# Tensor product pass: the edges of the first 136 destinations by dense one-hot sums, the gathered path in 42 rounds instead of 49

## The reference, cut to what matters

```python
h = jnp.maximum(_layernorm(x, axis=-1), 0.0)
x = x + _L1_gnn_ref(h, edge_index, edge_attr_9, L1_gnn_w0, ..., L1_gnn_w4)
...
summand = _tensor_product(x[i], edge_attr, [w0, w1, w2, w3, w4])     # i: source of the edge
out = jax.ops.segment_sum(summand, j, num_segments=x.shape[0])       # j: destination
```

## Time and profile before

| what | value |
|---|---|
| median of 3 executions | 5813.45 us (5812.42 to 5815.08) |
| span of the profiled execution | 5807.9 us; the median lies 5.55 us above it |
| busy over the span | PE 4154.3 us, DVE 2538.0, ACT 2396.3, POOL 4025.0 |
| tensor pass, first to last gather | 1036.8 to 2996.3 us |
| in that pass (1036 to 3010 us) | PE busy 1292.19 us, POOL 1481.96, DVE 411.88, ACT 379.40; granted clock of TensorE 0.78 |
| granted clock | mean 0.779 over the span |

### The profile page before, as it was taken

One profiled execution on the slowest core, in us unless ns is written; L12 is line 12 of the kernel. 1 busy time (PEld: TensorE's weight loads), 2 busy tenths in 40 slices (PEclk: granted clock), 3 DMA queues, 4 the chain that ended last, 5 costly groups with the idle time before them and its releaser, 6 DMA issues. The chain is left out here.

```text
span 5807.9 us, 96744 instructions
## 1 busy us (share of the span) xinstructions
PE 4154.3 (72%) x26855; PEld 3465.6 (60%) x26855; DVE 2538.0 (44%) x8212; ACT 2396.3 (41%) x5947; POOL 4025.0 (69%) x4127
## 2 busy tenths in 40 slices
PE   3299996566666666666666777777777777659995
PEld 2167664456656656565555666666666666546664
DVE  5898665212222222222235555555555555542224
ACT  1645554212112111121136776666666666530113
POOL 0267775677777777777756777777777777557774
PEclk7599997777778777778776767667666777679998
DMA  4134443222222222222223333333333333255552
GB/s 70 41 126 147 168 155 122 65 57 56 57 57 56 57 56 57 57 56 57 57 50 78 85 83 79 85 79 83 85 77 85 84 78 85 59 175 173 172 173 71
DMA packets 363883, 510.14 MB, mean 88 GB/s; under 512 B 200193, under 2 KB 258822, under 8 KB 352705
## 3 DMA queue, kind: packets, MB, share of 16 engines
q0 software_dynamic: 129536, 268.78, 18.2%
q1 hardware_dynamic: 231785, 238.76, 13.3%
q10 hardware_dynamic: 2400, 0.57, 0.1%
HBM read 416.50 MB, written 91.05 MB: 87 GB/s over the span
## 5 line engine op out<-in xcount | busy, mean ns | idle before, releaser
L3202 POOL DMA_INDIRECT rows_l<-table,idx_l x1568 | 1481.6, 945 | 511.5 <-issue 470.9
L2831 POOL DMA_INDIRECT rows_l<-table,idx_l x1568 | 1482.0, 945 | 497.2 <-issue 477.6
L1533 POOL DMA_INDIRECT rows_l<-table,row_idx x896 | 944.8, 1054 | 303.2 <-issue 271.8
L2972 PE MATMUL ps_l<-hoty_l,rows_l 128*128 128x144 f32 x3136 | 724.6, 366 | 335.8 <-DMA rows_l<-table,idx_l 278.8
L2852 ACT COPY agg_l<-ps_l 128x288 f32<-128x288 f32 x784 | 312.3, 398 | 1548.4 <-PE ps_l L2972 1547.7
L3490 PE MATMUL banks_l<-wrow_l,hot_l 128*128 128x136 f32 x3136 | 709.7, 397 | 276.5 <-ACT hot_l L3576 275.6
L3490 PEld LDWEIGHTS banks_l<-wrow_l,hot_l 128*128 128x128 f32 x3136 | 649.4, 296 | 343.9 <-issue 218.2
L2972 PEld LDWEIGHTS ps_l<-hoty_l,rows_l 128*128 128x128 f32 x3136 | 552.0, 239 | 417.5 <-DMA rows_l<-table,idx_l 268.3
L2898 DVE TENSOR_TENSOR hoty_l<-p_hot_l,y_l 128x1152 f32<-128x1152 f32 x196 | 266.0, 1357 | 913.8 <-PE ps_l L2972 803.0
L2987 PE MATMUL pm_l<-w_mix,agg_l 128*128 128x128 f32 x3528 | 637.4, 318 | 0.4 <-ACT msg_l L2863 0.4
L2987 PEld LDWEIGHTS pm_l<-w_mix,agg_l 128*128 128x128 f32 x3528 | 588.2, 235 | 7.5 <-ACT msg_l L2863 0.6
(11 more groups left out here) (565 smaller groups left out, 6992.9 us busy)
## 6 DMA issues: line engine op xcount, KB each, us to landing
rows_l<-table,idx_l POOLq DMA_INDIRECT x3136, 2.5
e_l<-in_edge_attr SPq DMA_DIRECT2D x196, 256.0 KB
counts_table<-x_nodes SPq DMA_DIRECT2D x22, 1568.0 KB
x_nodes<-counts_table SPq DMA_DIRECT2D x22, 1568.0 KB
counts_table<-h_nodes SPq DMA_DIRECT2D x21, 1568.0 KB
h_nodes<-counts_table SPq DMA_DIRECT2D x21, 1568.0 KB
rows_l<-table,row_idx POOLq DMA_INDIRECT x896
raw_l<-in_edge_attr SPq DMA_DIRECT2D x49, 144.0 KB
```

The source lines that it names most:

```text
L1533: pool.indirect_dma_start(out=rows[:, slot, j, :], out_offset=None, in_=table, in_offset=bass.IndirectOffsetOnAxis(ap=what[:, j:j + 1], ax ...
L2831: pool.indirect_dma_start(out=rows[:, u, j, :], out_offset=None, in_=table, in_offset=bass.IndirectOffsetOnAxis(ap=idx[:, u, j:j + 1], axi ...
L2972: last = nc.tensor.matmul(ps[q][:, at:at + Y * RANGE], rows[:, u, 2 * q + i, :], hoty[:, s, 2 * q + i, :, :].rearrange("p c d -> p (c d)") ...
L3202: pool.indirect_dma_start(out=rows[:, u, j, :], out_offset=None, in_=table, in_offset=bass.IndirectOffsetOnAxis(ap=idx[:, u, j:j + 1], axi ...
```

## The change

The first 28 groups (28,672 edges) are no longer gathered: the loop over groups runs over the last 168, now written out without a hardware loop (`PassGroup`). Instead the first 136 destinations are computed apart, 29,502 edges on average; of those past edge 28,672 the one-hot places in the gathered path are pushed out of range (`done_far`).

- A destination gets a fixed number of visits (`caps`, its mean count of edges plus 4.5 deviations, in tiles of 128): 22, 10, 8, 7, 6, 6, 5, ... 2, together 372 in 8 batches of 17 destinations (106, 52, 44 and five of 34).
- Two visits at a time, DVE makes one-hots of the source's low 7 bits (`d_hot`, 128x256) and of its high part (`d_high`, 128x98), and multiplies the latter by 9 attributes (`d_row`, 128x882). PE multiplies them (128x441 f32) and sums over the visits in the PSUM bank `pd`: this is the count of the destination over all 49x128 nodes for each attribute. ACT copies it to `d_sums`.
- For each batch 49 matmuls (128x153) with `core.h` in 7 slices sum h by those counts, ACT copies to `d_agg`, 9 small matmuls mix, DVE adds to `acc`.
- `plan` lays these pieces (372 visits, 56 slices, 8 mixes, 32 empty) over the 672 slots, from slot 32 to 12 before the end, at most one in a slot. The piece stands behind `sums` and `mix` of its slot on PE.
- SP loads sources and attributes of each destination by two DMAs (`load_dense`), one or several groups ahead. DVE prepares each batch by 22 small operations (`prepare`).
- A new small stage `dense_stage` works out where each destination's edges begin. If a destination has more edges than its visits hold, or the 136 have under 28,672, or edges are unsorted, the flag `num[0:1, 0:1]` makes the pass run twice, first over groups 28 to 195, then over 0 to 167, and the dense part counts nothing.
- The node stage of layer 1 writes to `core.h` in place of a double buffer `tab`.
- `pw` and `py` share a bank, so `turn_raw` is one piece in slot 0 of a round's second group, and `y` has two buffers.

```diff
+    NODES, BATCH, SKIP = 136, 17, 7
+    RUN, RING, SLICES, FIRST, TAIL = 2, 6, 7, 32, 12
...
+        self.caps = []
+        for i in range(self.NODES):
+            many = sh.e * (((i + 1) / sh.n) ** 0.5 - (i / sh.n) ** 0.5)
+            self.caps.append(int(-(-(many + 4.5 * many ** 0.5) // P)))
...
+        pieces, gaps = [], 0
+        for b in range(self.batches):
+            for i in range(b * self.BATCH, (b + 1) * self.BATCH):
+                for v in range(self.first[i], self.first[i + 1]):
+                    pieces.append(("visit", i, v))
+            pieces.append(None)
+            for k in range(self.SLICES):
+                pieces.append(("apply", b, k))
+            pieces.append(None)
+            pieces.append(("mix", b, 0))
+            pieces += [None, None]
+        self.groups = (self.sh.rounds - self.SKIP) * U
+        self.parts = J // 2
+        slots = self.groups * self.parts
+        room = slots - self.FIRST - self.TAIL
+        assert len(pieces) <= room
+        self.at = [[] for _ in range(slots)]
+        for n, piece in enumerate(pieces):
+            if piece is not None:
+                self.at[self.FIRST + n * room // len(pieces)].append(piece)
...
+            link(nc.vector.tensor_tensor_scan(ends[:, :], ones[:, :], many[:, :], 0.0, ALU.mult, ALU.add))
+            nc.vector.tensor_tensor(begins[:, :], ends[:, :], many[:, :], ALU.subtract)
...
+            nc.vector.tensor_scalar(num[0:1, 1:2], ends[0:1, N - 1:N], float(dense.skipped) - 0.5, None, ALU.is_lt)
+            link(nc.vector.tensor_scalar(num[0:1, 2:3], core.order[0:1, 1:2], 0.5 * FAR, None, ALU.is_lt))
+            link(nc.vector.tensor_tensor(num[0:1, 0:1], num[0:1, 0:1], num[0:1, 1:2], ALU.max))
...
+            nc.vector.tensor_scalar(num[0:1, 3:4], num[0:1, 0:1], -1.0, 1.0, ALU.mult, ALU.add)
...
+            def load_dense(w, i):
+                k = dense.caps[i]
+                first = dense.place_of(dense.first[i])
+                cols = slice(first, first + k)
+                if i % B == 0 and dense.batch_of(i) >= 2:
+                    sp.wait_ge(dense_hot, START + w * (V // RUN) + dense.columns(dense.batch_of(i) - 2).stop // RUN)
+                    sp.sem_inc(batch_begun, 1)
+                at = ds(sp.value_load(dense.starts[0:1, i:i + 1], min_val=0, max_val=sh.e - dense.most * P), k * P)
+                loaded = dense_loaded[dense.batch_of(i)]
+                sp.dma_start(d_src[:, cols], src[at].rearrange("(p j) -> p j", j=k)).then_inc(loaded, DMA)
+                sp.dma_start(d_attr[:, cols, :].rearrange("p j c -> p (j c)"),
+                             attr[at, :].rearrange("(p j) c -> p (j c)", j=k)).then_inc(loaded, DMA)
...
+            def take_dense(w, slot):
+                for kind, n, k in dense.done_before(slot):
+                    if kind == "visit" and k == dense.first[n + 1] - 1:
+                        act.wait_ge(dense_counted, START + w * V + k + 1)
+                        if n >= B:
+                            act.wait_ge(batch_applied, START + w * dense.batches + dense.batch_of(n))
+                        nc.scalar.copy(d_sums[:, :, :, n % B].rearrange("p a c -> p c a"),
+                                       pd[:, 0:wide].rearrange("p (c a) -> p c a", a=A)).then_inc(node_taken, 1)
+                    if kind == "apply" and k == dense.SLICES - 1:
...
+                        if n:
+                            act.wait_ge(batch_mixed, START + w * dense.batches + n)
+                        nc.scalar.copy(d_agg[:, :], pd[:, 0:Y * B]).then_inc(batch_taken, 1)
...
+            def hots_of_nodes(v, w):
+                at, mine = v % RING, dense.place_of(v)
+                if v >= RING:
+                    dve.wait_ge(dense_counted, START + w * V + v + RUN - RING)
+                dve.wait_ge(dense_hot, START + w * (V // RUN) + v // RUN)
+                nc.vector.tensor_tensor(d_high, steps[:, 0:A].unsqueeze(1).broadcast_to([P, RUN, A]),
+                                        d_hi[:, mine:mine + RUN].unsqueeze(2).broadcast_to([P, RUN, A]), ALU.is_equal).then_inc(dense_high, 1)
+                nc.vector.tensor_tensor(d_hot[:, at:at + RUN, :], steps.unsqueeze(1).broadcast_to([P, RUN, P]),
+                                        d_lo[:, mine:mine + RUN].unsqueeze(2).broadcast_to([P, RUN, P]), ALU.is_equal)
+                dve.wait_ge(dense_high, START + w * (V // RUN) + v // RUN + 1)
+                nc.vector.tensor_tensor(d_row[:, at:at + RUN, :, :], d_high.unsqueeze(2).broadcast_to([P, RUN, Y, A]),
+                                        d_attr[:, mine:mine + RUN, :].unsqueeze(3).broadcast_to([P, RUN, Y, A]), ALU.mult).then_inc(dense_hot, 1)
...
+            def turn_raw(t, k):
+                pe.wait_ge(raw_loaded, START + t * DMA + DMA)
+                if k is not None:
+                    pe.wait_ge(added, START + k)
+                pe.sem_inc(turn_begun, 1)
+                for c in range(Y):
                     last = nc.tensor.transpose(py[:, c * tiles:(c + 1) * tiles],
                                                raw[:, :].rearrange("t (e c) -> t c e", c=Y)[:, c, :], core.ident[0:tiles, 0:tiles])
-                if end == Y:
-                    last.then_inc(raw_turned, 1)
+                last.then_inc(raw_turned, 1)
...
+            def count_visit(w, i, v):
+                if v == dense.first[i]:
+                    if i:
+                        pe.wait_ge(node_taken, START + w * N + i)
+                    if i % B == 0 and dense.batch_of(i):
+                        pe.wait_ge(batch_added, START + w * dense.batches + dense.batch_of(i))
+                if v % RUN == 0:
+                    pe.wait_ge(dense_hot, START + w * (V // RUN) + v // RUN + 1)
+                nc.tensor.matmul(pd[:, 0:wide], d_hot[:, v % RING, :], d_row[:, v % RING, :, :].rearrange("p c a -> p (c a)"),
+                                        start=(v == dense.first[i]), stop=(v == dense.first[i + 1] - 1)).then_inc(dense_counted, 1)
...
+            def apply_batch(w, b, k):
+                first, end = A * k // dense.SLICES, A * (k + 1) // dense.SLICES
+                if k == 0:
+                    pe.wait_ge(node_taken, START + w * N + (b + 1) * B)
+                for a in range(first, end):
+                    last = nc.tensor.matmul(pd[:, 0:Y * B], core.h[:, a, :], d_sums[:, a, :, :].rearrange("p c i -> p (c i)"),
+                                            start=(a == 0), stop=(a == A - 1))
+                if end == A:
+                    last.then_inc(batch_applied, 1)
...
+            def dense_part(w, slot):
+                for kind, n, k in dense.at[slot]:
+                    if kind == "visit":
+                        count_visit(w, n, k)
+                    elif kind == "apply":
+                        apply_batch(w, n, k)
+                    else:
+                        mix_batch(w, n)
+            with pe.Fori(0, windows) as w:
+                turn_raw(w * R, None)
+                for g in groups_of(w):
                     for q in range(PAIRS):
-                        mix(g, q)
-                    place_sums(g.near(-1))
...
-                edge_loop(sh, pe, w, body)
+                        sums(g, q)
+                        mix(g.near(-1), q)
+                        if q == 1:
+                            place_sums(g.near(-2))
+                        if q == 0 and g.u == 1 and g.rnd < R - 1:
+                            turn_raw(g.t + 1, g.near(-3).k + 1 if g.near(-3) else None)
+                        dense_part(w, slots(g)[q])
+                    if g.near(1) is None:
+                        for q in range(PAIRS):
+                            mix(g, q)
+                        place_sums(g.near(-1))
+                        place_sums(g)
```

More of the change, by code:

```diff
@@ L2714, in tensor_pass @@
         tiles = U * J
-        full, rest = divmod(sh.e - (R - 1) * U * GROUP, P)
-        assert 0 < full < tiles and tiles == 32
+        full, rest = divmod(sh.e - (sh.rounds - 1) * U * GROUP, P)
+        assert 0 < full < tiles and tiles == 32 and R % 2 == 0
+        V, B, N, RUN, RING = dense.visits, dense.BATCH, dense.NODES, dense.RUN, dense.RING
+        seen, skipped_tiles = dense.seen_tiles, dense.SKIP * U * J
+        A = sh.blocks
+        wide = Y * A
+        assert wide <= 512 and Y * B <= 512
         rel = sb("rel", [P, G, J])
@@ new lines, in mix_batch @@
+            def mix_batch(w, b):
+                pe.wait_ge(batch_taken, START + w * dense.batches + b + 1)
+                for c in range(Y):
+                    last = nc.tensor.matmul(pd[:, 0:B], w_mix[:, c, :], d_agg[:, c * B:(c + 1) * B], start=(c == 0), stop=(c == Y - 1))
+                last.then_inc(batch_mixed, 1)
+            def dense_part(w, slot):
[6 more added lines that the diff above has]
+                        mix_batch(w, n)
```

473 lines of the change are left out of this document (347 added, 126 removed).

## The result

| | median of 4 executions | lowest to highest |
|---|---|---|
| before | 5812.93 us | 5808.65 to 5815.08 |
| changed | 5538.39 us | 5536.97 to 5545.04 |

The ratio is 0.9531, 95% interval 0.9517 to 0.9545: faster by 274.5 us. The forecast was 5547 us, range 5536 to 5600. The span of the profiled execution is 5536.5 us (before 5807.9), the mean granted clock 0.812 (0.779).

What follows compares the result with a forecast made beforehand. POOL's back-to-back gathers were taken to set the pass, all else beside them. Terms -280 + 8 + 3 + 0 + 1 + 2 = -266 us took the span from 5807.9 to 5541.9; plus 5.55 gave 5547 us, range 5536 to 5600.

Steps and rivals of the forecast that it cites:

- The bound and the main term: Pass: POOL's gathers set the time; 224 fewer gathers at 1.250 us each save 280.0 us.
- PE fits: Pass: PE's 1147 us at full clock plus 70 of waits fit POOL's 1680 us, at a clock of 0.8 or more.
- Waits: Pass: PE waits for ACT's copy out of `pd`, 0.66 us at 135 places, 0 to 89 us, taken as 70.
- `raw`: PE's wait for attributes each round grows from 6.9 to 9.4 us, less for a late PE; it costs nothing.
- DVE: Pass: a pair of visits takes 1.75 us; DVE needs 721 of 1680 us in all and stays hidden.
- POOL disturbed: Pass: DVE's small preparations lengthen the gathers they meet, 0 to 5 us, taken as 2 us.
- Fixed costs: Outside the gathers: `dense_stage` 8 us (5 to 15), start of the pass 3 (1 to 7), end 0.
- A backlog of PE at the end: End of the pass: dense work left on PE could last to the end, 1 us, bounds 0 to 12.
- The sum: Whole kernel: the terms add to -266 us, span 5541.9 us; with 5.55 us from span to median, 5547 us.
- PE behind in part: Rival in the pass: at clock 0.70 PE needs 1728 us against 1680, 48 us more, 5595 us; chance 15%.
- the half clock rival: Rival in the pass: PE at half clock becomes the bound, about 2530 us, total 6397 us; chance 3%.
- The pass ran once: Rival on the whole pass: the flag fires and the pass runs twice, 7227 us; chance 1%.

Runs made afterwards that it cites:

- 41, 42 and 44 rounds: Gathered rounds: 41 is the changed kernel taken to 187 destinations, 5502.29 us; 42 the changed kernel, 5538.39 us; 44 has two rounds given back, 5627.07 us.
- the kernels with other orders: `d_sums` reordered so ACT writes adjacent elements: changed kernel 5543.75 us; 187 destinations 5539.44 us; 187 destinations with matmuls reading runs of 9, ratio 0.9466.
- twice the visits: Changed kernel with each visit's matmul issued two times into the same sum: 5542.87 us, ratio 0.9532.
- the matmuls read with a step, at 187 destinations: 187 destinations, 41 rounds, with sums ordered so ACT writes adjacent elements and matmuls read at a stride: 5539.44 us, against 5502.29 us in the changed kernel's order.
- three times the visits: Changed kernel with each visit's matmul issued three times into the same sum: 5749.54 us, ratio 0.9888.

## Why the prediction was right

- **The bound and the main term.** -280.0 us were forecast for 224 gathers at 1.250 us. First to last gather is 279.1 us shorter, and leaving the whole dense part out makes it 1.3 us shorter still and no more. The same price holds for 41, 42 and 44 rounds: 1.2505, 1.2506 and 1.2500 us a gather.
- **PE fits.** 1147 us of work were forecast, and the clock to rise to 0.8 or more; it is 0.88. What the forecast had as "80 to 90% busy" is 77%: the clock's rise took back what the added work put in, and with the waits for `raw` it was enough. The margin is known from the runs: 279 us more hide, 558 us more don't. Between these no run lies.
- **Waits.** ACT's copy: 0 to 89 us, taken as 70, is 72.6. That agreement is partly luck. The copy itself was estimated at 0.61 us and takes 0.97, so a wait is 0.86 us in the mean (72.6 / 84) and not 0.66; but it occurs at 84 places of 135 and not at nearly all. The cause of the 0.97, the output's step, was shown by the kernels with other orders.
- **`raw`.** The account holds. The wait was to grow from 6.9 us to 9.4 by standing a slot earlier, and to shrink for a PE that comes late, to under 6.9 in the mean. Without the dense part it is 9.25 us; with it 6.9 (281.7 / 41, and 272.9 / 40 = 6.8 from 1100 us on), by which the two effects just cancel, so "shorter" holds by no more than 0.1 us. With twice the visits 2.9 us are left (61 / 21). The 7.4 us in the text of the run with 44 rounds is 309.5 / 42 and takes in the 27.8 us at the start of the pass, which the 6.9 leaves out.
- **DVE.** A pair of visits was forecast at 1.75 us and takes 0.26 + 0.41 + 1.07 = 1.74. DVE's whole share, forecast as 721 of 1680 us, is 686 of 1694.
- **POOL disturbed.** 2 us, bounds 0 and 5. The busy time exceeds 1344 x 0.944 = 1268.7 by 2.4 us, and leaving the dense part out shortens the gathers by 1.3. The rule of the Trainium skill's "SBUF — State Buffer", section "Who interferes with whom", gave up to 27 us. The runs don't bear that out: the trace shows a tenth of it, and 996 copies of 294 ns cost 10 us where the expectation by that rule was 150 to 200. That the price was right is in part luck: it was taken from the sum pass's 0.11 us a gather, and nothing here shows that this is the cause at work.
- **Fixed costs.** `dense_stage` 8 us, measured 6.2; start of the pass 3, measured 2.4 (7.46 - 5.05); end 0, measured 0. A backlog of PE at the end 1, measured 0.7 (from the last gather to the last `acc` 12.6 us in place of 11.9). Together 8 + 3 + 0 + 1 = 12 forecast for 9.3.
- **The sum.** -266 forecast, -271.4 in the spans. The terms give -279.1 + 6.2 + 2.4 + 0.7 = -269.8. The remaining -1.6 us lie in the stages between and behind, where runs of kernels with equal code there differ by more. Of the 9 us by which the median lies under the forecast (5538.4 for 5547.4), 5.4 are in this sum. The other 3.7 were no part of the change: the forecast added 5.55 us from span to median, as in the kernel before, and here the median lies 1.9 us above the profiled span.
- **The rivals.** PE behind in part did not occur with 397 us of dense work, but its mechanism is real: it comes with the matmuls read with a step, at 187 destinations (+37 us), and with three times the visits (+211). In both the granted clock is 0.95 or more, not the 0.70 on which I had priced it. The argument against it in the prediction, that a PE that falls behind doesn't idle and gets the full clock, is what the rows show. With it the half clock rival falls too. The pass ran once: 1344 gathers.
- **A slip in a rival.** The argument for a PE behind in part gave a slice of 7 matmuls 0.91 us at full clock and 1.9 at half. That counts one record a matmul; there are two, as the sum of 102 us rightly has it. The trace shows a slice twice as long:

```profile
1895.37 2.00 PE L3371 MATMUL pd_l<-d_sums_l,h_nodes 128*128 128x153 f32 x14
1897.20 0.65 PE L3322 MATMUL ps_l<-hoty_l,rows_l 128*128 128x144 f32 x4
...
1910.44 3.92 PE L3371 MATMUL pd_l<-d_sums_l,h_nodes 128*128 128x153 f32 x14
1914.17 0.68 PE L3322 MATMUL ps_l<-hoty_l,rows_l 128*128 128x144 f32 x4
```

From start to start 1.83 us at full clock, and 3.73 us behind a wait for `raw`, at half clock. With the 0.94 us of `sums` and `mix` a slot with a slice is longer than its 2.5 us even at full clock. PE makes up for it in the slots without a piece, which take it 0.93 us (the sums start at 1900.19 and 1901.12 us), and POOL waits only when PE is more than three groups behind; no such wait is seen. The rival had more for it than its text says.

## What to carry to other kernels

When one engine's issue rate sets a stage, take work away from its queue and put it on engines that wait for it, even where it is more arithmetic: here 28,672 edges moved at the cost of some 9 us beside the gathers. Ask of the receiving engine what it needs at full clock plus the waits that then are no longer hidden, not what it is busy now; its busy share barely moves as the clock rises. When two engines share a buffer, look for the order in which both touch runs of adjacent elements: each side alone can be made fast at the other's cost.

## What the runs showed of the hardware

- ACT's copy of 128x441 f32 from PSUM to SBUF takes 970 ns when the elements that it writes one after the other lie 153 elements (612 bytes) apart, and 533 ns with adjacent output. A source in PSUM with a step of 49 elements costs nothing: 532 ns.
- A f32 matmul record over 153 columns takes 293 ns with adjacent columns, 455 ns with columns 441 elements (1764 bytes) apart, and 296 ns with runs of 9 adjacent columns. I hadn't expected either step to cost this much. The Trainium skill, "SBUF — State Buffer", section "Door 1: The DMA port swizzle", says that SBUF has lines of 16 bytes and that each access that crosses to a new line pays for it. These runs agree in kind, for the matmuls and for ACT's output; the page gives no size, and no run separates lines from steps. The same place says that any access to PSUM that isn't adjacent slows matmuls; no run here has a matmul with such an access. For ACT's read of PSUM, of which the page doesn't speak, no slowing is seen (532 ns).
- DVE copies of 256 f32 elements, SBUF to SBUF (294 ns), lengthened the gathers' chain by 10 ns each. A gather's own record went from 946 to 953 ns in the mean.
- In this pass the granted clock followed PE's work: 0.76, 0.88, 0.96 and 0.98 with no, one, two and three times the dense visits. PE busy moved only from 62% (1047 of 1694 us) over 77% and 90% to 93%. The busy share alone doesn't give the clock: in layer 2's pass of the changed kernel PE is busy 74% (1411 of 1900 us) at a clock of 0.72.
- An engine that is held up can show it as "issue" and not as a wait: 570.3 us of issue with a longest of 5.7 us, where an undisturbed POOL has 409.3 with 0.3.
